# Query, key and position parts gathered into their stacks inside SBUF instead of through DRAM

## The reference

```python
x = x + _layernorm(_L0_attn_ref(_layernorm(x), ...))   # layer norm, GRU of width 256 over 512 steps, projection
x = x + _layernorm(_L0_ffn_ref(_layernorm(x), ...))    # 8 experts by LoRA, top-1 gate
x = x + _layernorm(_L1_attn_ref(_layernorm(x), ...))   # 16 heads of 16, see below
x = x + _layernorm(_L1_ffn_ref(_layernorm(x), ...))    # SwiGLU, hidden 384, integer weights
```

```python
proj = layer_norm(x) @ W_in.T + b_in
q, k, v, p, y = split(proj, [256, 512, 768, 1024])     # q, k, v: 16 heads of 16
k = (1 - smear) * k + smear * k_prev                   # key of the token before
pos = cumsum(sigmoid(y))                               # one position per head
scores = (q / s) @ (k / s).T / 4 + causal - (pos[i] - pos[j])
o = softmax(scores) @ v
out = layer_norm((silu(p) * o) @ W_out.T)
```

## Time and profile before

| | us |
|---|---|
| median of three executions | 1505.95 |
| lowest and highest of them | 1502.7, 1507.28 |
| the profiled execution, device time | 1511.65 |
| span of the profiled execution, first to last instruction | 1509.4 |

### The profile page before, as it was taken

How to read it: one execution, slowest core, us unless ns; L and a number is a source line. 1 busy time by engine, 2 the same in 40 slices (tenths; PEclk the granted TensorE clock), 3 DMA queues, 4 the chain that set the end, 5 groups by cost and what they waited for, 6 DMA issues and landing times. The chain is left out here.

```text
span 1509.4 us, 64193 instructions
## 1 busy us (share of the span) xinstructions
PE 1299.7 (86%) x26361; PEld 971.4 (64%) x26361; DVE 1151.1 (76%) x5180; ACT 855.4 (57%) x2991; POOL 403.3 (27%) x754
## 2 busy tenths in 40 slices
PE   5888888888888888888888885589999999999986
PEld 4677777777777777777777774245555555555543
DVE  5778888888888888888888885867677677677475
ACT  3555555444555445554555552347777777777864
POOL 2101111111111111111111112552553553522454
PEclk9999999999999999999999996779999999999998
DMA  5200000000000000000000000394662672660001
GB/s 121 40 4 6 6 7 5 6 7 5 6 7 6 5 7 6 7 5 6 7 6 5 7 5 8 100 145 88 111 108 49 108 108 51 106 88 1 2 21 35
DMA packets 68937, 53.60 MB, mean 36 GB/s; under 512 B 12686, under 2 KB 68390, under 8 KB 68646
## 3 DMA queue, kind: packets, MB, share of 16 engines
q1 hardware_dynamic: 66470, 49.32, 19.0%
q10 hardware_dynamic: 2176, 0.20, 0.1%
HBM read 31.84 MB, written 15.47 MB: 31 GB/s over the span
## 5 line engine op out<-in xcount | busy, mean ns | idle before, releaser
L759 PE MATMUL PS<-GQ,W 128*128 128x32 f16 x12288 | 497.0, 177 | 103.1 <-DVE GQ L1127 87.4
L759 PEld LDWEIGHTS PS<-GQ,W 128*128 128x128 f16 x12288 | 415.8, 96 | 207.2 <-DVE GQ L1127 199.7
L1012 ACT ACTIVATE RQ<-PS 128x16 f32<-128x16 f32 x512 | 102.6, 200 | 342.3 <-PE PS L759 342.1
L2564 DVE TENSOR_REDUCE MX<-PS 128x1 f32<-128x512 f32 (+3 forms) x352 | 218.8, 634 | 87.1 <-PE PS L2005 85.1
L2290 ACT ACTIVATE PT<-PS 128x512 f32<-128x512 f32 (+1 forms) x352 | 193.3, 566 | 104.3 <-PE PS L2021 101.1
L1118 DVE TENSOR_TENSOR_SCAN PS<-RQ,PS 128x64 f32<-128x64 f32 x512 | 151.3, 295 | 81.8 <-ACT RQ L1012 68.8
L828 PE MATMUL PS<-W 128*128 128x256 f16 x1024 | 196.2, 273 | 0.0
L1001 ACT ACTIVATE GB<-GQ 128x32 f16<-128x32 f16 x512 | 171.8, 336 | 0.4 <-DVE GQ L1132 0.4
L718 POOL TENSOR_TENSOR rt<-mv,eps 128x1 f32<-128x1 f32 x93 | 17.8, 192 | 500.9 <-DVE mv L1141 500.9
L1014 ACT ACTIVATE ZB<-PS 128x16 f32<-128x16 f32 x512 | 95.2, 186 | 90.2 <-PE PS L759 90.1
L2002 PE MATMUL PS<-KS,QS 99*128 99x256 bf16 (+3 forms) x512 | 133.7, 313 | 11.0 <-DVE MX L2564 9.2
(11 more groups left out here) (487 smaller groups left out, 2836.5 us busy)
## 6 DMA issues: line engine op xcount, KB each, us to landing
QS<-q_parts SPq DMA_DIRECT2D x90, 128.0 KB, 9.6
KS<-k_parts SPq DMA_DIRECT2D x90, 128.0 KB, 12.4
q_parts<-PQ SPq DMA_DIRECT2D x16, 384.0 KB, 10.2
k_parts<-PK SPq DMA_DIRECT2D x16, 384.0 KB, 3.2
X<-XM SPq DMA_DIRECT2D x32, 64.0 KB
out_dram<-X SPq DMA_DIRECT2D x8, 256.0 KB, 2.3
XM<-in_L_attn_x_dram SPq DMA_DIRECT2D x16, 80.0 KB
s_hh<-in_L_attn_w_hh_dram SPq DMA_DIRECT2D x1, 768.0 KB, 5.8
```

Of the source, the lines that this page charges most:

```text
L759: return pe.matmul(bank[:, p, at:at + WIDE].rearrange("p (r b) -> p r b", b=B), W[:, kc, w:w + P], state[:, kc, :, part].unsqueeze(1).to_b ...
L2564: dve.tensor_reduce(MX[:, g % 2, heads[0]:heads[-1] + 1, NT - 1 - it], p_x[:, k % 2, 0:len(heads) * w].rearrange("p (a w) -> p a w", w=w), ...
```

## The change

Attention: the three tensors in DRAM are gone. For every sequence and every group g of four heads, SP issues one transfer for each of the six query blocks and six key blocks straight from `PQ` and `PK` (64 rows of 1 KB) to 16 rows of the stack (4 KB each), and one for the position rows: 13 for a group, 52 for a sequence. So that the 64 source rows of a group come in the order of the stack, the rows of the weights for q and k are loaded permuted (`s_in` in nine transfers instead of one, `bqk` in eight instead of one), and the columns of `KA`, `sel8` follow. Each group has a semaphore of its own (`group_in`); a group of sequence b may be overwritten when that group's scores of b - 2 are done. POOL may overwrite a half of `PQ` or `PK` when the two groups of that half have landed in the stacks of the sequence before (`stacked`).

```diff
 def project(b, p):
+    for c in range(2):
+        sp.wait_ge(parts_q.sem, parts_q.value(sp, b, 4 * (c + 1)))
+        sp.wait_ge(parts_k.sem, parts_k.value(sp, b, 4 * (c + 1)))
+        if c == 0:
+            sp.wait_ge(kaT.sem, kaT.value(sp, b))
+        for g in (2 * c, 2 * c + 1):
+            if b >= 2:
+                sp.wait_ge(e_ps.sem, e_ps.value(sp, b - 2, NI * (g + 1)))
+            stack_extra(p, g)
+            stack(QS, PQ, Q_ORDER, p, g)
+            stack(KS, PK, K_ORDER, p, g)
...
 def project_first():
+    sp.wait_ge(parts_q.sem, 4)
+    stack(QS, PQ, Q_ORDER, 0, 0)
+    sp.wait_ge(parts_k.sem, 4)
+    stack(KS, PK, K_ORDER, 0, 0)
+    stack(QS, PQ, Q_ORDER, 0, 1)
+    sp.wait_ge(kaT.sem, kaT.value(sp, 0))
+    for g in range(NG4):
+        stack_extra(0, g)
+    stack(KS, PK, K_ORDER, 0, 1)
+    sp.wait_ge(parts_q.sem, parts_q.value(sp, 0))
+    for g in (2, 3):
+        stack(QS, PQ, Q_ORDER, 0, g)
+    sp.wait_ge(parts_k.sem, parts_k.value(sp, 0))
+    for g in (2, 3):
+        stack(KS, PK, K_ORDER, 0, g)
+def stack(dst, src, order, p, g):
+    rows = slice((g % 2) * 4 * DH, (g % 2 + 1) * 4 * DH)
+    for r, part in enumerate(order):
+        sp.dma_start(dst[r * DH:(r + 1) * DH, p, 4 * g:4 * g + 4, :].rearrange("d h n -> d (h n)"),
+                     src[rows, g // 2, part, :]).then_inc(group_in[p][g].sem, 16)
...
 # POOL
+def stacked(b, c):
+    if b:
+        for g in (2 * c, 2 * c + 1):
+            done = group_in[1 - b % 2][g]
+            hold(pool, done.sem, done.value(pool, (b - 1) // 2))
 def split(b, i):
-            if not (isinstance(b, int) and b == 0):
-                hold(pool, q_out.sem, q_out.before(pool, b))
+            stacked(b, c)
...
 # PE
 def stacks(b, p, g):
+    if b == 0 and g == 0:
+        pe.wait_ge(ones_in.sem, ones_in.value(pe, 0))
+    pe.wait_ge(group_in[p][g].sem, group_in[p][g].value(pe, b // 2))
```

```diff
 # ACT
-col(gam[:, :], gamma_d, 1)
+act.dma_start(gam[:, :], ...).then_inc(loads_late.sem, 16)
+for j in range(2):
+    load_unit(act, j, loads_x0)
...
-act.activation(flat(W1), flat(whhT), ACT.Copy, scale=S_gru).then_inc(high_w.sem, 1)
+for kc in range(HC):
+    act.activation(W1[:, kc, :], whhT[:, kc, :], ACT.Copy, scale=S_gru).then_inc(high_w.sem, 1)
 # DVE, behind the maximum of s_hh
+dve.wait_ge(loads_x0.sem, 32)
 for j in range(2):
     dve.bn_stats(STb[:, j, :], XM[:, j, :]).then_inc(stats.sem, 1)
...
+dve.wait_ge(loads_ih.sem, 16)
 dve.tensor_reduce(mx[:, 1:2], flat(s_ih), AX.X, ALU.max, apply_absolute_value=True)
-dve.wait_ge(loads_gb.sem, 64)
+dve.wait_ge(loads_late.sem, 16)
 dve.tensor_reduce(mx[:, 2:3], gam[:, 0:1], AX.X, ALU.max, apply_absolute_value=True)
...
-dve.tensor_tensor(wb[:, :, :], s_ih[:, :, :], bet ..., ALU.mult)
 # POOL, behind row_scales
+pool.tensor_tensor(wb[:, :, :], s_ih[:, :, :], bet ..., ALU.mult)
```

More of the change, by code:

```diff
@@ L238, in load_x, with load_unit @@
             eng.dma_start(XM[t * B:(t + 1) * B, first:last, :], x_by_step[t][:, first:last, :]).then_inc(done.sem, 16)
+        def load_unit(eng, j, done):
+            eng.dma_start(XM[:, j, :], x_by_step[:, :, j, :]).then_inc(done.sem, 16)
         ctx = ExitStack()
@@ L310, in build @@
             N_F = 5 + FC + 4
[L311 removed]
+            N_LATE = 30
             @block.gpsimd
@@ L396, in _ @@
                 col(bhh[:, :], b_hh_d, 6)
-                for t in range(1, GS, 2):
-                    load_x(act, t, 0, X_FIRST, loads_x0)
+                for j in range(2, X_FIRST):
+                    load_unit(act, j, loads_x2)
                 act.wait_ge(consts.sem, 2)
@@ L482, in _ @@
                 dve.tensor_tensor(BP[:, :, 2], BR[:, :], BP[:, :, 1], ALU.subtract).then_inc(bias_v.sem, 1)
[L483 to L485 removed]
+                for kc in range(HC):
+                    dve.wait_ge(high_w.sem, kc + 1)
+                    dve.scalar_tensor_tensor(W2[:, kc, :], whhT[:, kc, :], S_gru, W1[:, kc, :], ALU.mult, ALU.subtract).then_inc(low_w.sem, 1)
+                dve.wait_ge(high_w.sem, HC + 1)
                 dve.scalar_tensor_tensor(V2[:, :], wihT[:, :], S_gru, V1[:, :], ALU.mult, ALU.subtract).then_inc(low_w.sem, 1)
@@ L681, in row @@
                     sp.dma_start(dst, src.partition_broadcast(P)).then_inc(loads_late.sem, 16)
-                sp.dma_start(s_in[:, :, :], w_in_d[0:4 * DE, :].rearrange("(c p) k -> p c k", p=P)).then_inc(loads_late.sem, 16)
+                for c in range(2 * DE // P):
+                    for a in range(2):
+                        rows = w_in_d[c * P + a * 4 * DH:c * P + (a + 1) * 4 * DH, :]
+                        sp.dma_start(s_in[a * 4 * DH:(a + 1) * 4 * DH, c, :], rows.rearrange("(h d) k -> d h k", d=DH)).then_inc(loads_late.sem, 16)
+                sp.dma_start(s_in[:, 2 * DE // P:, :], w_in_d[2 * DE:4 * DE, :].rearrange("(c p) k -> p c k", p=P)).then_inc(loads_late.sem, 16)
                 sp.dma_start(s_iny[:, :], w_in_d[4 * DE:, :]).then_inc(loads_late.sem, 16)
@@ L689, in _ @@
                     load_x(sp, t, X_FIRST, X_NEXT, loads_x)
-                col(bqk[:, :], b_in_d[0:2 * DE], 4)
+                by_group = b_in_d[0:2 * DE].rearrange("(c a h d) -> c a d h", c=4, a=2, d=DH)
+                for c in range(4):
+                    for a in range(2):
+                        sp.dma_start(bqk[a * 4 * DH:(a + 1) * 4 * DH, c:c + 1], by_group[c, a],
+                                     allow_slow_non_contiguous=True).then_inc(loads_late.sem, 16)
                 col(ilw[:, :], in_ln_w_d, 1)
@@ L1524, in build @@
             kaT = signal("kaT_ready")
[L1525 to L1529, removed]
+            group_in = [[signal(f"stack_{p}_group_{g}_in", 16 * 13) for g in range(4)] for p in range(2)]
             s_ps = signal("score_ps", NI * NG4)
@@ L1669, in project @@
[L1669 to L1678, removed]
@@ L1711, in _ @@
                 sp.wait_ge(ones_set.sem, 1)
-                for p, done in ((0, first_in[0]), (1, stack_in[1])):
-                    sp.dma_start(QS[96:KM, p, :, :], onesb[:, :].unsqueeze(1).to_broadcast([KM - 96, HEADS, S])).then_inc(done.sem, 16)
+                for p in range(2):
+                    sp.dma_start(QS[96:KM, p, :, :], onesb[:, :].unsqueeze(1).to_broadcast([KM - 96, HEADS, S])).then_inc(ones_in.sem, 16)
                 project_first()
-                project(1, 1)
-                with sp.Fori(1, B // 2) as q:
-                    for p in range(2):
-                        project(sp.snap(q * 2 + p), p)
+                for b in range(1, B):
+                    project(b, b % 2)
@@ L1742, in split @@
                         hold(pool, kk2.sem, kk2.value(pool, b, c + 1))
-                        if not (isinstance(b, int) and b == 0):
-                            hold(pool, k_out.sem, k_out.before(pool, b))
+                        stacked(b, c)
                     pool.tensor_copy(dst[:, c, 0, :], src[:, c, :]).then_inc(parts.sem, 1)
@@ L1915, in project_qk @@
                         for t in range(NT):
-                            last = pe.transpose(p_k[:, t * P:(t + 1) * P], KA[:, t, :, :].rearrange("p h r -> p (h r)"), identb[:, :])
+                            last = pe.transpose(p_k[:, t * P:(t + 1) * P], KA[:, t, :, :, :].rearrange("p g r h -> p (g r h)"), identb[:, :])
                         last.then_inc(kaT_ps.sem, 1)
```

143 lines of the change are left out of this document (51 added, 92 removed).

## The result

The changed kernel takes 1532.0 us (median of 4, 1530.4 to 1535.4), the kernel before 1504.6 (median of 4 beside it, 1502.7 to 1507.3). The ratio is 1.0178, with a 95% interval from 1.0155 to 1.0200: 27.4 us slower. The forecast was 1514, its range ended at 1524. The side was right, the size was not.

The account below looks back on a forecast made before the run. PE was taken as busy nearly throughout, with time to change only at its standstills in the first block and the attention's beginning. 1505.95 + 7.4 + 4.0 - 3.5 gave 1514; the forecast's own range was 1509 to 1523, overall 1502 to 1524.

Parts of the forecast that it names:

- What bounds the kernel: Whole attention: PE is busy 183.77 of 200 us; the trip through DRAM is hidden in seven bodies of eight.
- Rival 3: Later bodies gain from a third less DMA traffic: 1507 at 1 us per body, 1495 without POOL's waits; chance 0.12.
- My sign for it: Later bodies: PE's idle share falling below 8% would show the prediction wrong.
- The beginning of the attention: POOL's second query split of sequence 1 waits for 52 landings; PE's row-maximum transpose begins 7.4 us later (5.8 to 10.0).
- the first 18 transfers: Sequence 0: 18 of 52 transfers stand ahead of the position rows, issued while SP would wait for these anyway.
- body(0): POOL's second query split of sequence 2 waits 6.5 us; PE stands 4.0 us (1.6 to 8.3).
- From body(1) on: Remaining bodies: the last 13 transfers land in time, six us before POOL's second split, so no wait.
- The first block: Before the GRU: waits for x and gam go and wb leaves DVE, 3.5 us gained (2.0 to 4.3).
- The second: Rival: DMA engines set the pace at 0.63 us a transfer (1523), or PE's clock falls (1520 to 1529); chance 0.13.
- The other leg: PE's clock falls to 1.2 GHz after a 4 us stop in body(0), costing some 6 us more: 1520 to 1529.
- Rival 1: New transfers issue faster, 0.34 us each; POOL's first wait costs 2.2 us, its second nothing: 1504.6; chance 0.20.

Follow-up runs that it names:

- the kernel with two sets: The changed kernel with two sets of the part buffers PQ, PK and KAT, for even and odd sequences: 1504.1 us, ratio to the kernel before 1.0006.
- the first block alone: The kernel before with only the first block's part of the change (x by unit, wb on POOL, DVE order, gamma's semaphore): 1501.1 us, ratio 0.9988.

## Why the prediction was wrong, point by point

**What bounds the kernel: right.** Nothing on PE's side waited for the trip through DRAM. With the holds gone, the kernel with two sets takes what the kernel before takes, in spite of all that traffic less. Rival 3, a gain in the bodies, gave nothing: in the 200 us from 1100 PE is busy for 184.33 with two sets, at 58 GB/s, and for 184.28 with the first block alone, which still goes through DRAM at 95 GB/s. My sign for it, an idle share of PE below 8% in the later bodies, came out at 7.5% all the same, and means nothing: the window of the earlier trace rows holds the two stretches at a low clock.

**The beginning of the attention: the mechanism right, the term too small.** The split waited for the landings, `QA` stood behind it, and PE behind `QA`, as written; the landing came 1.98 us behind the last issue (1.8 put), and split and `QA` took 5.41 us (5.5 put). The term that failed is the price of an issue. I took 0.51, the mean of a row of the same kind (`X<-XM`, 0.55, with its gap 0.60) and of one from DRAM (0.46); it was 0.63. For a position transfer I took 0.37 from `k_extra`, a plain block; it was 0.80. By the forecast's own sum, 30 x 0.12 + 4 x 0.43 = 5.3 us more; 0.7 more come from the first 18 transfers, which I called free: SP was not done with them when the position rows were ready (965.28, by ACT's timeline) and began the first of these at 965.95. 7.4 + 5.3 + 0.7 = 13.4, and 13.8 was measured. That bytes don't set the price of an issue could have been read in SP's timeline of the kernel before (2.77 us for six reads of 64 KB and of 128 KB).

**body(0): the same term.** 48 x 0.12 + 4 x 0.43 = 7.5 us, and 1.8 us in single issues that were held up: 35.2 us a sequence in place of 26.0. 4.0 + 9.2 = 13.2, and 13.4 was measured.

**From body(1) on: right on PE, but with less in hand.** I had 6 us to spare; POOL waited 1.41 in body(1) and nowhere behind it. PE's list of waits for the whole attention has two for `QA`, and these are the two above.

**The first block: 1.9, not 3.5**, just under its lower end. DVE still waited 0.81 us for `x`, of the 2.62 of the earlier trace rows, and `wb`, which I put on POOL beside DVE's work at nothing, drew out a DVE step by 1.45 us. No row that I had read could show that. The Trainium skill has the rule: in "SBUF — State Buffer", section "Who interferes with whom", a DVE instruction with two SBUF inputs waits for a POOL instruction that reads SBUF, for its whole length. The trace agrees, with 1.60 against 0.15 us for a step that began 0.21 us behind `wb`, and with `wb` back on DVE the stretch is gone.

**The rivals.** The second had two legs. That the DMA engines set the pace at 0.63 us, by the 104 GB/s of the Trainium skill ("SBUF — State Buffer", section "Door 1: The DMA port swizzle"), gave 1523 and met the time of a transfer by chance: it was SP that took 0.63, with the engines at a share of 0.28, and when they were the bound they moved 125 to 141 GB/s into blocks of 16 partitions, six blocks in turn, and not 104; no run streams into one block alone. The other leg happened: behind the second stop PE ran at the 1.2 GHz level and lost 2.6 us, where I had put some 6 for a stop that I thought shorter. Legs that I kept apart came together with a forecast that was itself too small, and the range had no place for the sum. Rival 1 put the issue at 0.34; it was nearly double.

**The range** ended where its own upper price, 0.60, ended; the sum with that price and with 2.0 for the first block is 1505.95 + 10.0 + 8.3 - 2.0 = 1522.3, not 1523. The nearest row for SBUF to SBUF was that end; I took a mean with a row of another kind and so moved away from the better evidence. With 0.60 in both waits the forecast would have been 1520.8.

## What to carry to other kernels

Price a transfer by its count first: here an issue from SBUF into 16 partitions took 0.63 us for 16 KB, 64 KB and 128 KB alike, so a queue's time is issues times that, until the bytes fill the engines. Tell the two apart by the DMA share: in these runs 0.28 with a queue that issues without a break is the issuer, 1.1 and more is the engines; but 0.28 doesn't mean room for three times as much: that queue moved 96 GB/s, and full engines moved 125 to 141. And when a change makes a buffer free later, ask which engine waits for it in order, and what stands behind it there; a second buffer gave back 27.9 us without one transfer less.

## What the runs showed of the hardware

- The issue time goes neither by bytes nor simply by source or form: 0.42 us from DRAM into 16 partitions, 0.59 from SBUF into 16, 0.59 from either into 64, 0.67 for 32 rows into 8, 0.76 for 24 rows into 6 (the gap of 0.04 not counted).
- One queue of 64 KB transfers into 16 partitions moved 96 GB/s at a share of 0.28; 128 KB a transfer 125 GB/s at 1.14; two queues 130 to 141 at 1.17 to 1.18.
- A [1, 1] step on DVE took 1.60 us in place of 0.15 beside a POOL product of 1.80 us, a 128 x 128 step 2.24 in place of 0.33 beside the same product, and four steps of 128 x 512 4.7 in place of 2.2 beside POOL's split.
